# Second cross-attention of a two-layer block: 32-row score tiles, zero products between, five units squared on GpSimd

## What is computed

```python
rq = (iQ @ Wq.T).reshape(b, q, H, ADIM)
kv = (iK @ Wkv.T).reshape(b, s, 2, H, ADIM)
rk, rv = (kv[:, :, 0], kv[:, :, 1])
scores = jnp.einsum('bqhd,bshd->bhqs', rq, rk) / sqrt(ADIM)
scores = jnp.where(mask[:, None, :, :], jnp.float32(-1e+32), scores)
t = jax.nn.relu(scores + nbias[0])
t = t * t
attn = t / (t.sum(-1, keepdims=True) + 1e-32)
o = jnp.einsum('bhqs,bshd->bqhd', attn, rv).reshape(b, q, H * ADIM)
return o @ Wo.T
```

## Time and profile before

| | us |
|---|---|
| median of 3 runs | 424.77 |
| lowest, highest | 423.61, 426.24 |
| the profiled execution | 423.58 |
| its span, first to last instruction | 421.8 |
| TensorE, VectorE, ScalarE, GpSimd busy | 389.5, 329.5, 261.2, 229.0 |
| mean granted clock of TensorE | 0.991 |

### The profile page before, as it was taken

How to read it: one execution, slowest core, us unless ns; L and a number is a source line. 1 busy time by engine, 2 the same in 40 slices (tenths; PEclk the granted TensorE clock), 3 DMA queues, 4 the chain that set the end, 5 groups by cost and what they waited for, 6 DMA issues and landing times.

```text
span 421.8 us, 8012 instructions
## 1 busy us (share of the span) xinstructions
PE 389.5 (92%) x3110; PEld 317.9 (75%) x3110; DVE 329.5 (78%) x492; ACT 261.2 (62%) x382; POOL 229.0 (54%) x139
## 2 busy tenths in 40 slices
PE   8987999999998999999898888999599999976996
PEld 6765899999997899999897566864366666654795
DVE  3799888898987888987562656997798988953764
ACT  3576788777778778777661355110189989953343
POOL 0032889999779987886430500870097775600034
PEclk9999999999999999999999999999889999999999
DMA  6948877887998778887498003994610000010000
GB/s 201 270 123 199 195 179 177 193 190 178 214 213 176 173 174 183 194 183 167 127 393 322 0 2 62 213 225 100 257 62 2 3 3 2 3 34 0 2 0 14
DMA packets 20014, 57.04 MB, mean 135 GB/s; under 512 B 6528, under 2 KB 8104, under 8 KB 18312
## 3 DMA queue, kind: packets, MB, share of 16 engines
q1 hardware_dynamic: 19976, 56.53, 53.7%
HBM read 18.63 MB, written 0.13 MB: 44 GB/s over the span
## 4 chain that ended last, share of the span: by engine, by line
PE 67%; DVE 11%; SPq 6%; ACT 5%; DMA 5%; issue 4%; POOL 2%; POOLq 0%; ACTq 0%; DVEq 0%
PE ps L948 7%; PE ps L969 6%; PE ps L670 6%; PE ps L672 5%; PE ps L671 5%; PE ps L648 5%; PE ps L649 5%; PE ps L650 5%; SPq L521 4%; PE ps L1042 4%; PE ps L902 3%; PE ps L911 3%; DVE max L1499 3%; DVE y_sq L1489 2%; DMA wkvo_sb<-in_wkvo 2%
## 5 line engine op out<-in xcount | busy, mean ns | idle before, releaser
L390 POOL TENSOR_TENSOR dT_lo<-z_sq,dT_hi 128x1024 fp32r<-128x1024 f32 x56 | 133.3, 2400 | 31.3 <-ACT dT_hi L1071 31.2
L1136 ACT ACTIVATE y_sq<-ps,nmax 128x1024 f32<-128x1024 f32 x64 | 70.8, 1113 | 40.9 <-DVE nmax L1528 38.6
L1499 DVE TENSOR_REDUCE max<-ps 128x1 f32<-128x1024 f32 x64 | 77.9, 1218 | 20.0 <-PE ps L650 19.9
L670 PE MATMUL ps<-dT_hi,ctx_hi 128*128 128x256 f32 x256 | 74.3, 290 | 2.1 <-POOL dT_lo L390 2.1
L1489 DVE STREAM_TRANSPOSE y_sq<-y_sq 128x1024 f32<-128x1024 f32 x60 | 74.0, 1234 | 0.0
L672 PE MATMUL ps<-dT_hi,ctx_lo 128*128 128x256 f32 x256 | 72.4, 283 | 0.0
L671 PE MATMUL ps<-dT_lo,ctx_hi 128*128 128x256 f32 x256 | 72.3, 283 | 0.0
L1646 DVE SCALAR_TENSOR_TENSOR w_ring<-ps,mask_sb 128x1024 f32<-128x1024 f32 x54 | 63.0, 1219 | 5.5 <-PE ps L948 4.3
L1071 ACT ACTIVATE dT_hi<-z_sq 128x1024 fp32r<-128x1024 f32 x60 | 61.5, 1059 | 2.7 <-PE ps L672 2.5
L1268 ACT ACTIVATE p_ring<-w_ring 128x1024 f32<-128x1024 f32 x54 | 55.9, 1056 | 4.5 <-DVE w_ring L1646 2.6
L648 PE MATMUL ps<-ctxT_hi,qk_hi 128*128 128x512 f32 x128 | 52.5, 410 | 4.0 <-ACT y_sq L1136 3.6
(11 more groups left out here) (212 smaller groups left out, 627.5 us busy)
## 6 DMA issues: line engine op xcount, KB each, us to landing
z_sq<-y_sq SPq DMA_DIRECT2D x240, 128.0 KB, 2.4
w_sb<-in_w SPq DMA_DIRECT2D x2, 2048.0 KB, 14.9
kstack<-k_hi SPq DMA_DIRECT2D x16, 256.0 KB, 5.0
ctx_raw<-in_ctx_nat SPq DMA_DIRECT2D x8, 256.0 KB, 8.2
ctxT_raw<-in_ctx_t SPq DMA_DIRECT2D x1, 2048.0 KB, 7.7
kstack<-k_lo SPq DMA_DIRECT2D x8, 256.0 KB, 5.0
wg_sb<-in_wg SPq DMA_DIRECT2D x1, 1088.0 KB, 4.8
wu_sb<-in_wu SPq DMA_DIRECT2D x1, 1088.0 KB, 7.1
```

The costliest lines, as they stand in the source:

```text
L390: return engine.tensor_tensor(d_ring(dT_lo, m), z_chunk(m), d_ring(dT_hi, m), ALU.subtract)
L670: mm(acc, hi[:, k, :], dT_hi[m % 3][:, cols], start=(k == 0), stop=False)
L1136: nc.scalar.activation(out_t, keys, ACT.Exp, bias=nmax[:, hs % 2:hs % 2 + 1], scale=SCALE0, accum_out=rowsum[:, hs, p:p + 1]).then_inc(exp ...
L1499: return v.tensor_reduce(max2[:, 2 * (hs % 2) + p:2 * (hs % 2) + p + 1], slot(2 * hs + p), AX.XY, ALU.max)
```

## The change

- Scores: `kstack` and the new `q_rows` hold four rows per head dimension side by side (high key with high q, low key with high q, high key with low q, and a row of ones with the bias), 32 rows per head. A pair of units takes 16 products of 32 rows by 128 by 128 columns, four row groups writing to four banks; the banks of both must have been read before it starts. The two units of a pair are now the two halves of the heads for the same keys (`combo`, `block_of`). `wkvo1`'s key columns are put in that order by four transfers of 32-byte pieces, beside one for the rest.
- Ones: GpSimd fills one group's columns early (128 x 4096), six transfers copy them to the other groups.
- q: GpSimd spreads `wq1` fourfold (`wq1_rows`); eight products; VectorE makes batch entry 0's rows with three operations; ScalarE copies entry 1's product out, and GpSimd makes its rows with four operations between the first side units. The row kinds come from five small reductions of the identity on VectorE; small operations on GpSimd that made the bias rows move and change.
- Zeros: eight idle products before `turn_xn(3)`, five after the q products (`keep_busy`), and, in the loop, eight products of zeros added into the same sums after every value product at an odd place of WEIGHED that is no side unit, nor first or last of its combination. The sums of both batch entries stand side by side in banks 6 and 7, cleared earlier; two copies instead of four.
- Side units are now 0, 6, 12, 18, 24, 32, 38, 44, 50, 56. Five further units (POOLED) are masked by VectorE into a place of their own and squared by GpSimd there, after the side unit before them; they too stand 5.5 places later in WEIGHED.
- `wq_mla`, `wk_mla` change places in memory with others, as the ones come earlier.

```diff
-        UNITS = NBLK
         COMBOS = B * 2
-        NU = COMBOS * UNITS
-        SIDE = tuple(range(0, NU - 6, 6))
+        NU = COMBOS * NBLK
+        SIDE = tuple(range(0, 25, 6)) + tuple(range(32, 57, 6))
+        POOLED = (27, 35, 41, 47, 53)
         SIDE_LAG = 5
+        BUSY = 2
...
+        def ring_nth(m):
+
+            return main_nth(m) - sum(k <= m for k in POOLED)
+
+        def pooled_nth(m):
+
+            return POOLED.index(m) + 1
...
+        RING = [m for m in MAIN if m not in POOLED]
+        WEIGHED = sorted(range(NU), key=lambda m: m + SIDE_LAG + 0.5 if m in SIDE or m in POOLED else m)
...
+        def combo(m):
+
+            return m // (2 * NBLK) * 2 + m % 2
+
+        def block_of(m):
+
+            return m % (2 * NBLK) // 2
...
-            get(wkvo1[:], "wkvo1", "l1w")
+            get(wkvo1[:, 1:3, :], "wkvo1", "l1w", ins["wkvo1"][:, 1:3, :])
+            for g in range(4):
+                get(wkvo1[:, 0, HR * g:HR * g + HR].rearrange("p (r d) -> p r d", r=4), "wkvo1", "l1w",
+                    ins["wkvo1"][:, 0, :].rearrange("p (r g d) -> p g r d", r=4, g=4)[:, g, :, :])
...
+            sp.wait_ge(ones_done, 1)
+            for b in range(B):
+                for g in range(3):
+                    keys = slice(b * CTX, (b + 1) * CTX)
+                    sp.dma_start(kstack[3:P:4, g, keys].bitcast(F32), kstack[3:P:4, 3, keys].bitcast(F32))\
+                        .then_inc(ones_in[b], 16)
...
-                for t in (0, 2, 1):
+                for t in range(3):
                     part = k1_lo if t == 1 else k1_hi
-                    sp.dma_start(kstack[32 * t:32 * t + 32, g, keys].bitcast(F32),
-                                 part[32 * g:32 * g + 32, keys].bitcast(F32)).then_inc(kstack_in[i], 16)
+                    sp.dma_start(kstack[t:P:4, g, keys].bitcast(F32),
+                                 part[HR * g:HR * g + HR, keys].bitcast(F32)).then_inc(kstack_in[i], 16)
...
+            def keep_busy(count):
+
+                for _ in range(count):
+                    mm(ps[:, 7, T:2 * T], zeros[:, 0:P], zeros[:], start=True, stop=True)
...
-            pe.wait_ge(load["wq1"], 16)
+            pe.wait_ge(acc_zero, 1)
+            keep_busy(8)
+            pe.wait_ge(wq1_laid, 4)
             turn_xn(3)
-            for g in range(4):
-                last = mm(ps[:, 2 + g // 2 * 2, (g % 2) * T:(g % 2 + 1) * T], wq1[:, g, :], xnT[:],
-                          start=True, stop=True)
-                if g % 2:
-                    last.then_inc(q1_psum, 1)
+            for b in range(B):
+                for g in range(4):
+                    last = mm(ps[:, 2 + 2 * b, g * S:(g + 1) * S], wq1_rows[:, g, :], xnT[:, b * S:(b + 1) * S],
+                              start=True, stop=True)
+                last.then_inc(q1_psum, 1)
+            keep_busy(5)
+
+            def slot_read(m):
+
+                if m in SIDE:
+                    pe.wait_ge(relu_done, side_nth(m))
+                else:
+                    pe.wait_ge(w1_done, main_nth(m))
 
             def scores1(m):
 
-                c, k = m // UNITS, m % UNITS
-                b = c // 2
-                if m >= 3:
-                    if m - 3 in SIDE:
-                        pe.wait_ge(relu_done, side_nth(m - 3))
-                    else:
-                        pe.wait_ge(w1_done, main_nth(m - 3))
-                if m == 0:
-                    pe.wait_ge(ones_done, 1)
+                b, k = m // (2 * NBLK), block_of(m)
+                for i in range(2):
+                    if m + i >= 3:
+                        slot_read(m + i - 3)
                 if m == 2:
-                    pe.wait_ge(q1s_done, 2)
-                for a in range(2):
-                    g = 2 * (c % 2) + a
+                    pe.wait_ge(q1b_read, 1)
+                if k == 0:
+                    pe.wait_ge(q_made[b], 1)
+                    pe.wait_ge(ones_in[b], 48)
+                at = b * CTX + k * P
+                for g in range(4):
                     if k == 0:
-                        if 4 * b + g >= 2:
-                            pe.wait_ge(qbd_pool, 4 * b + g - 1)
-                        else:
-                            pe.wait_ge(qbd_done, g + 1)
                         pe.wait_ge(kstack_in[4 * b + g], 48)
-                    at = b * CTX + k * P
-                    last = mm(ps[:, 2 * (m % 3) + a, :], kstack[:, g, at:at + P],
-                              qbd[:, b, g, :, :].rearrange("p h s -> p (h s)"), start=True, stop=True)
-                last.then_inc(s1_psum, 1)
+                    for r in range(4):
+                        rows, bank = slice(HR * r, HR * r + HR), 2 * ((m + r // 2) % 3) + r % 2
+                        last = mm(ps[:, bank, g * S:(g + 1) * S], kstack[rows, g, at:at + P], q_rows[rows, b, g, :],
+                                  start=True, stop=True)
+                        if g == 3 and r % 2:
+                            last.then_inc(s1_psum, 1)
...
             def weigh_v(m):
 
 
-                c, k = m // UNITS, m % UNITS
+                c, k = combo(m), block_of(m)
                 b, n = c // 2, weighed_nth(m)
-                first = n == min(weighed_nth(i) for i in range(c * UNITS, (c + 1) * UNITS))
-                if first and c >= 2:
-                    pe.wait_ge(o1_copied, c - 1)
+                first, final = n == min(of_combo(c)), n == max(of_combo(c))
                 if m in SIDE:
                     pe.wait_ge(sq_pool, side_nth(m))
                     p = p_side[:]
+                elif m in POOLED:
+                    pe.wait_ge(pooled_done, pooled_nth(m))
+                    p = w_pooled[:, (pooled_nth(m) - 1) % 2, :]
                 else:
-                    pe.wait_ge(sq_done, main_nth(m))
-                    p = p_ring[:, (main_nth(m) - 1) % 3, :]
+                    pe.wait_ge(sq_done, ring_nth(m))
+                    p = p_ring[:, (ring_nth(m) - 1) % 3, :]
                 for a in range(2):
                     for j in range(4):
                         pair = (b * NBLK + k) * H // 2 + 4 * (c % 2) + j
-                        last = mm(ps[HR * j:HR * j + 2 * (DA + 1), 6 + c % 2, 0:S],
+                        last = mm(ps[HR * j:HR * j + 2 * (DA + 1), 6 + c % 2, b * S:(b + 1) * S],
                                   v1[:, pair, a:a + 2, :].rearrange("p w d -> p (w d)"),
                                   p[:, (2 * j + a) * S:(2 * j + a + 1) * S],
-                                  start=first and a == 0, stop=n == combo_weighed(c) and a == 1)
+                                  start=first and a == 0, stop=final and a == 1)
+                if n % 2 and m not in SIDE and not first and not final:
+                    for _ in range(BUSY):
+                        for j in range(4):
+                            last = mm(ps[HR * j:HR * j + 2 * (DA + 1), 6 + c % 2, b * S:(b + 1) * S],
+                                      zeros[:, 0:2 * (DA + 1)], zeros[:, 0:S], start=False, stop=False)
                 last.then_inc(pv1_done, 1)
...
             for m in range(0, NU + WEIGH_LAG + 1, 2):
-                for i in range(2):
-                    if m + i < NU:
-                        scores1(m + i)
+                if m < NU:
+                    scores1(m)
...
+            act.wait_ge(q1_psum, 2)
+            copy(q_raw[:].rearrange("p g s -> p (g s)"), ps[:, 4, :]).then_inc(q1b_read, 1)
...
+                if m not in RING:
                     continue
-                at = main_nth(m)
-                act.wait_ge(w1_done, at)
+                at = ring_nth(m)
+                act.wait_ge(w1_done, main_nth(m))
                 if at > 3:
-                    act.wait_ge(pv1_done, weighed_nth(MAIN[at - 4]))
+                    act.wait_ge(pv1_done, weighed_nth(RING[at - 4]))
                 nc.scalar.activation(p_ring[:, (at - 1) % 3, :], w_ring[:, (at - 1) % 3, :],
                                      ACT.Square).then_inc(sq_done, 1)
...
-            pool.wait_ge(mo_proj, 1)
-            pool.wait_ge(xm_done, E0 // 2)
-            nc.gpsimd.memset(kstack[96:128, :, :].rearrange("p g n -> p (g n)").bitcast(F32), 1.0).then_inc(ones_done, 1)
+            nc.gpsimd.memset(kstack[:, 3, :].bitcast(F32), 1.0).then_inc(ones_done, 1)
...
+                one = wq1[:].rearrange("p r (t q) -> p r t q", t=4)[:, :, 0, DA * g:DA * g + DA]
+                nc.gpsimd.tensor_scalar(wq1_rows[:, g, :].rearrange("p (r d t) -> p r d t", r=4, d=DA), bc(one, 3, 4),
+                                        1.0, None, ALU.mult).then_inc(wq1_laid, 1)
...
+                for k in POOLED:
+                    if m < k < m + 6:
+                        pool.wait_ge(w1_done, main_nth(k))
+                        w = w_pooled[:, (pooled_nth(k) - 1) % 2, :]
+                        nc.gpsimd.tensor_tensor(w, w, w, ALU.mult).then_inc(pooled_done, 1)
+                if n == 0:
+                    pool.wait_ge(q1b_read, 1)
```

(35 more changed lines are left out.)

106 lines of the change are left out of this document (45 added, 61 removed).

## The result

The changed kernel takes 434.1 us (median of four runs, 432.98 to 434.48) against 424.9 for the kernel before: ratio 1.020, 95% interval 1.016 to 1.024. It is slower, as forecast; the size was forecast as +7.5 us and is +9.2 by the medians, +9.4 between the two profiled executions (432.98 and 423.58), of which +9.1 lies in their spans (430.9 and 421.8).

The account below looks back on a forecast made before the run. TensorE was taken as the bound, at 6.37 us per six units. Entry -0.4, weight +1.5, first half +0.7, second half +5.6 and tail +0.1 gave +7.5: 423.58 to 431.1 us, range 419 to 436 (forecast's own 427.5 to 434).

Parts of the forecast that it names:

- The second half, +5.6: Loop from unit 32: late products of 37 make VectorE stand 1.9 us, period 7.8 against 6.37 us, four times: +5.6 us.
- VectorE alone bounds the stage: Rival for the second cross-attention: only 0.5 us stands remain, 63.5 us against 68.5, kernel faster at 419.8 us; chance 0.18.
- the products of 37: Second half: value products waiting for a late square, 0.50 us, ahead of scores (40,41), which start at 3.49 us.
- Scores at 0.50 us per pair: Loop: a pair's 16 products of 32 rows cost 0.50 us, with 0.3 and 0.86 as ends.
- First half, +0.7: Loop units 0 to 31: six units take 6.5 us against 6.37, VectorE waiting for ScalarE's chain; five groups, +0.7 us.
- Entry, -0.4: Way into the second cross-attention: first mask at 304.6 against 305.01 us; net -0.4 us, between -2 and +1.
- Saved and nearly given back: Entry: time lost by q products at the 1.2 GHz level is saved, but idle products delay transposes 1.2 us.
- The weight, +1.5: k1 weight in five transfers: 2048 small packets delay its landing, hence TensorE's fill, by 1.5 us (0 to 5.0).
- Two of the forecast's signs: Signs that would show the forecast right: fill starting at 232 to 233 us, first mask near 306 us.
- the estimate of 21.5 us: Weight transfers: the skill page's 10.5 ns per packet times 2048, making the sum 451; the forecast argued against it.
- only +0.1: Tail behind the loop: one copy of 256 columns for one of 128, +0.1 us.
- the lower level for the stage in a rival: Rival 'TensorE stays the bound': scores 0.86 us per pair, by serial weight loads or 1.2 GHz; about +12, 436 us; chance 0.13.

Follow-up runs that it names:

- run 1: Changed kernel with no units squared by GpSimd (POOLED empty, squares back on ScalarE): 1.003 of the kernel before.
- run 2: Changed kernel with only TensorE's value-product order altered: second-half side units 3.5 places later instead of 5.5; GpSimd keeps its five units: 1.006 of the kernel before.
- run 10: Changed kernel, stands included, with idle products filling TensorE's first score waits, behind the loop and in the following self-attention: 429.2 us, 1.009 of the kernel before.
- run 5: Changed kernel without GpSimd-squared units, idle products filling TensorE's first score waits, behind the loop and in the following self-attention: 0.993 of the kernel before.
- run 6: Changed kernel with only the value-product order altered (as run 2), plus the same filling of TensorE's waits as run 5: 0.997 of the kernel before.
- run 12: Kernel before the change, with TensorE's waits filled at the entry, behind the loop and in the self-attention: 0.993 of the unfilled kernel before.
- run 7: Changed kernel without the eight and five idle products at the entry of the second cross-attention: 1.025 of the kernel before.
- Run 8: Changed kernel with the k, v, o weight loaded in one transfer instead of five (scores of other columns, only times used): 1.020 of the kernel before.
- run 4: Changed kernel without the zero products beside the value products (BUSY = 0): 1.028 of the kernel before.
- run 9: Kernel before the change with only the entry filled: five idle products ahead of the third layer's transposes, four behind its q products: 1.000 of the kernel before.
- run 3: Changed kernel with four idle products put into TensorE's waits behind the loop only: 1.020 of the kernel before.
- run 11: run 5 less the zero products inside the loop: 0.994 of the kernel before.

## Why the prediction was right, and where it was not

*The second half, +5.6: right, and shown.* Four stands before units 40, 46, 52 and 58 were forecast at 1.9 us and are 2.0; the period was forecast at 7.8 and is 7.79. Runs 1 and 2 remove them in two ways, the second by TensorE's order alone, and run 10 shows that they stand without any help of the clock. It is the one term that makes the sign. That +5.1 came out and not +5.6 lies mostly in the kernel before: the same 24 units hold its group of 7.18 us (344.41 to 351.59), which the forecast took at 6.37 like the others.

*The rival 'VectorE alone bounds the stage'* needed the products of 37 not to hold the next scores. Runs 1 and 2 grant that, and the loop still takes 69.0 and 70.9 us, with filled waits 68.2 and 68.7 (runs 5 and 6), and not 63.5: the 0.6 us stand per group stays. Between a mask and the scores three units on lie one square, one side read and the pair's scores; with that chain a group of the first half takes the same 6.37 us that it took with TensorE's work before. So even without its stands the new form of scores gains nothing, which run 12 shows from the other side.

*Scores at 0.50 us per pair: a little low.* They take 0.60 to 0.65 on the chain, and zero products 0.44 per sixteen, not 0.50. On the stands two other errors cancel, by luck: the value products ahead of the scores take 0.64 us (355.44 to 356.08) where 0.50 was written, and from the first score to VectorE it is 0.65 (356.08 to 356.73) where 0.80 was.

*The page on the matrix engine.* The Trainium skill, "TensorE: Matmul & The Clock Gate", section "Measured speedup vs the span model", gives 3.07 times for four 32-row tiles (of 512 columns; here they have 128). The traces do not show that for this form: a pair's scores went from 1.12 to 0.65 us, 1.7 times.

*First half, +0.7: 0.7 too small, and its parts were others.* A group takes 6.37 us, not 6.5; instead the first eight units (first mask to the mask of unit 8) take 8.93 us where they took 7.52. In runs 5, 6 and 10, with the first waits filled and no stretch at 0.50, they take 8.03: so 0.9 of the 1.4 us is the 1.2 GHz level from 307.9 to 311.3, and 0.5 stays whatever the clock and belongs to the start of the new form.

*Entry, -0.4: right,* 73.40 against 73.79 us from the fill to the first mask. 'Saved and nearly given back' is what run 7 shows: from the last fill's start to the first mask it is 9.28 us without the idle products, 10.26 with them, 10.66 before the change.

*The weight, +1.5: wrong.* The step that failed is 2048 small packets priced from the earlier trace rows and added behind the landing of the earlier trace rows. Run 8 finds no such cost. Two of the forecast's signs failed with it: the fill starts at 230.81 and not at 232 to 233, the first mask at 304.21 and not near 306. In this trace the five transfers were in place when TensorE was done:

```profile
L501 SPq DMA_DIRECT2D wkvo_sb<-in_wkvo x5: 328/507/598, 223.9 to 226.0; - x5
...
DMA to landing us min/median/max: 4.2/4.7/4.8
```

(Tile wkvo_sb, changed kernel: ns least/median/most, first and last start; by these the last lands near 230.7, the single transfer before landed at 231.1.) The first part, now 128 KB, lands within 4.8 us where 192 KB took 7.27 us. The Trainium skill, "DMA: Bandwidth & Descriptors", section "Measured (HBM→SBUF, 128 partitions, SWDGE, issued from GpSimd)", puts about 10.5 ns on each packet of a small transfer, issued from GpSimd and not, as here, from SP; the estimate of 21.5 us by it is ruled out by the same two lines.

*The missing term, +3.3.* Behind the loop I carried only +0.1 and took all that follows as it was. The profile before had two hints that I read only for the entry: a granted clock of 0.50 in a stretch, and idle products of fixed number on the path, whose length grows at that level (2.76 to 4.94 us). I named the lower level for the stage in a rival, and not for what follows it.

The errors (-1.9 for the weight, +0.7 in the first half, +3.3 for the clock behind the loop, -0.5 in the second half) leave +1.6 of the 9.1: the total was close partly by luck, because the weight's error and the clock's go against each other.

*What stays open.* Which of several waits brings the lower level, and how much of its place is chance. With the same bare waits behind the loop the trace of the kernel before shows none of it, those of the changed one and of runs 4, 7, 8 and 9 two stretches, run 1 one and run 2 none. Code that no run changed has it in some traces only: k1's fill in runs 4 and 7, the products near 260 us in runs 7, 10 and 11, 27 to 33 us in run 12. So it is not shown that runs 3 and 9 moved a stretch by their filling. What the traces do show is that none is there in the five with all these waits filled (runs 5, 6, 10, 11, 12), and that the entry's (308 to 311 us) is in all seven traces of the new form with those waits bare (the changed kernel, runs 1 to 4, 7 and 8) and in none of the four with them filled.

## What to carry to other kernels

A unit taken off a busy engine must keep its place in the in-order queue of the engine that consumes it: here two units put back by the same distance pulled the next ones ahead of work that others waited for, and one sort key was worth as much as the whole loss in the loop. Before an engine's work is shortened, walk the chain that will end last afterwards; here TensorE's 6.37 us per group gave way to a chain through ScalarE of the same 6.37 us. And compare any gain with the kernel before under the same granted clock: filling the waits at the entry and behind the loop with idle products left the old and the new scores (these without the stands) the same 0.7% under the kernel before.

## What the hardware showed that was not expected

- Filling some of TensorE's waits can be worth nothing: runs 3 (1.020) and 9 (1.000) gained nothing, and in their traces the filled place is at 2.4 GHz and a later one, with bare waits, at 1.2 (in run 3, 12 idle products 2.76 instead of 4.94 us, then 16 of them 5.97 instead of 4.77). Which of the bare waits are hit differs from trace to trace.
- Sixteen products of 32 rows by 128 columns, on four row groups, take 0.60 to 0.65 us in a row, 1.7 to 1.9 times as fast as four of 128 rows by 512 columns (1.12).
- One transfer of 192 KB took 6.7 to 7.7 us to land (four traces); cut into 128 KB and four parts of 16 KB in 32-byte pieces, each part landed 3.8 to 5.1 us after its issue (ten traces), and the last of them in the changed kernel's trace no later than the one before the change.
